# Four graph layers on one core: the scaled table rows of layers 1 and 2 made by ACT, tile by tile, in place of Pool's products

## What is computed

```python
edge_index = jnp.stack([src, dst])
x = _layernorm(x + _L0_gnn_ref(x, src, dst, edge_weight), axis=-1)
x = _layernorm(x + _L1_gnn_ref(x, src, dst, ...), axis=-1)
x = _layernorm(x + _L2_gnn_ref(x, src, dst), axis=-1)
x = _layernorm(x + _L3_gnn_ref(x, edge_index, ...), axis=-1)
```

```python
# layer 1: _gcn_conv, then a mixture of experts and a batch norm
norm = inv_sqrt[edge_src] * inv_sqrt[edge_dst]
agg = segment_sum(feats[edge_src] * norm[:, None], edge_dst)
# layer 2
xs = x * norm_in[:, None]
h = segment_sum(xs[s], d) * norm_out[:, None]
```

## Time and profile before

| | |
|---|---|
| median of 3 runs | 7959.14 us (7951.74 to 7964.05) |
| the profiled execution | 7969.68 us, span in the profile 7968.1 us |
| TensorE clock granted, mean | 0.811 |
| PE busy / POOL busy | 5263.4 us (66%) / 5261.4 us (66%) |
| DVE busy / ACT busy | 3827.5 us (48%) / 1977.2 us (25%) |
| boundary 1 | from about 3270 to 3349 us |
| boundary 2 | from about 5446 to 5549 us |

### The profile page before, as it was taken

How to read it: one execution, slowest core, us unless ns; L and a number is a source line. 1 busy time by engine, 2 the same in 40 slices (tenths; PEclk the granted TensorE clock), 3 DMA queues, 4 the chain that set the end, 5 groups by cost and what they waited for, 6 DMA issues and landing times. The chain is left out here.

```text
span 7968.1 us, 132980 instructions
## 1 busy us (share of the span) xinstructions
PE 5263.4 (66%) x33652; PEld 3720.9 (47%) x33653; DVE 3827.5 (48%) x17654; ACT 1977.2 (25%) x5480; POOL 5261.4 (66%) x4303
## 2 busy tenths in 40 slices
PE   0666666666666675088888447801888884888885
PEld 0555555555555454055444446600554443554444
DVE  4876667776777674622322553325223225223225
ACT  1333334444444442411110002302111002110003
POOL 0788888888888887266666552275666664666663
PEclk5898888898888886598899558955889985889987
DMA  9677777777667775666654105613455543455542
GB/s 213 59 74 69 72 74 82 83 89 92 95 98 101 101 105 66 227 199 210 190 168 148 34 31 155 173 45 102 150 154 168 165 156 106 151 159 164 168 153 81
DMA packets 942951, 982.36 MB, mean 123 GB/s; under 512 B 203852, under 2 KB 825779, under 8 KB 942538
## 3 DMA queue, kind: packets, MB, share of 16 engines
q0 software_dynamic: 309984, 274.81, 27.1%
q1 hardware_dynamic: 286252, 521.11, 20.6%
q10 hardware_dynamic: 346302, 181.56, 8.2%
HBM read 622.06 MB, written 337.58 MB: 120 GB/s over the span
## 5 line engine op out<-in xcount | busy, mean ns | idle before, releaser
L756 POOL DMA_INDIRECT work<-table,src_t x2169 | 2203.5, 1016 | 1127.7 <-issue 631.8
L789 POOL DMA_INDIRECT sums<-work,idx x1564 | 2478.5, 1585 | 690.8 <-issue 289.8
L1296 PE MATMUL pp<-shared 128*128 128x408 bf16 (+7 forms) x10584 | 2191.3, 357 | 703.2 <-issue 354.9
L1296 PEld LDWEIGHTS pp<-shared 128*128 128x128 bf16 x10584 | 1053.9, 105 | 1678.0 <-issue 854.0
L1727 DVE TENSOR_TENSOR acc<-acc,pp 128x80 f32 x543 | 128.4, 237 | 1921.3 <-remote 1283.0
L1278 PE MATMUL pp<-work 128*128 128x80 f32 x4338 | 659.6, 297 | 245.9 <-issue 134.3
L1278 PEld LDWEIGHTS pp<-work 128*128 128x128 f32 x4338 | 649.5, 216 | 326.1 <-issue 282.1
L1193 PE MATMUL pp<-acc 128*128 128x130 f32 x3128 | 536.8, 324 | 326.8 <-ACT work L944 269.4
L1193 PEld LDWEIGHTS pp<-acc 128*128 128x128 f32 x3128 | 469.8, 229 | 344.9 <-issue 344.9
L1015 ACT ACTIVATE shared<-shared 128x128 bf16<-128x128 f32 x588 | 179.2, 305 | 1693.3 <-DVE shared L1734 723.2
L961 ACT ACTIVATE shared<-pp 128x441 bf16<-128x441 f32 (+18 forms) x1086 | 547.4, 550 | 111.5 <-PE pp L1232 77.3
(11 more groups left out here) (316 smaller groups left out, 7105.8 us busy)
## 6 DMA issues: line engine op xcount, KB each, us to landing
shared<-counts SPq DMA_DIRECT2D x84, 840.0 KB
shared<-counts SPq DMA_DIRECT2D x42, 882.0 KB
work<-table,src_t POOLq DMA_INDIRECT x2169
shared<-counts SPq DMA_DIRECT2D x42, 819.0 KB
shared<-counts SPq DMA_DIRECT2D x42, 808.5 KB
shared<-counts SPq DMA_DIRECT2D x42, 798.0 KB
shared<-counts SPq DMA_DIRECT2D x42, 756.0 KB
shared<-counts SPq DMA_DIRECT2D x42, 714.0 KB
```

The lines of the kernel that those rows point to most:

```text
L756: pool.indirect_dma_start(out=msg[:, i % SLOTS, k, :], out_offset=None, in_=table, in_offset=bass.IndirectOffsetOnAxis(ap=src_t[:, at:at + ...
L789: pool.indirect_dma_start(out=sums0[k], out_offset=bass.IndirectOffsetOnAxis(ap=picked, axis=0), in_=rows, in_offset=None, bounds_check=NP ...
L1296: i = pe.matmul(bank[c][:, 0:COLS[n]].rearrange("p (k w) -> p k w", w=PACK * w), x3[:, b % 2, h, part3, :], ring[:, q % RING, 0:TB * COLS[ ...
```

## The change

Pool's `scale_rows` is taken out. ACT gets a new stage `scaled_rows`, which makes the same rows with seven activations of 128x128 (a Copy with a scale per partition) in place of the one product of 128x896. In ACT's order it stands one batch late, behind `deviation`: a step of ACT is now `normal_rows(b-1)`, `deviation(b)`, `scaled_rows(b-1)`. It waits for the same two signals as before, X of its batch (now ACT's own work) and the store that used the slot last. Pool has nothing left to do at boundary 1. At boundary 2 it has `shift` alone, and only two of its steps are written out ahead of its loop.

```diff
@@ Pool
-            def scale_rows(layer, scale):
-
-                def body(b, s, turn):
-                    pool.wait_ge(x_ready, layer * NB + b + 1)
-                    pool.wait_ge(tab_stored[s], 16 * ((layer + 1) * STORES + turn))
-                    pool.tensor_tensor(slot[:, 2 + s, :, :], X[:, tiles(b), :],
-                                       in_scale[:, scale, tiles(b)].unsqueeze(2).to_broadcast([P, TB, D]), ALU.mult).then_inc(tab_ready, 1)
-                return body
...
             extra_windows(pool, scatter_extra)
-            batches(pool, scale_rows(0, 0))
             gather(1)
...
-            batches(pool, shift, scale_rows(1, 1), lags=(0, 1))
+            batches(pool, shift)
@@ ACT
+            def scaled_rows(layer):
+
+                def body(b, s, turn):
+                    apart(act, x_ready, layer * NB + b + 1)
+                    act.wait_ge(tab_stored[s], 16 * ((layer + 1) * STORES + turn))
+                    for j in range(TB):
+                        i = act.activation(slot[:, 2 + s, j, :], X[:, b * TB + j, :], ACT.Copy,
+                                           scale=in_scale[:, layer, ds(b * TB + j, 1)])
+                    i.then_inc(tab_ready, 1)
+                return body
...
-            batches(act, normal_rows(0, 0), deviation(0), lags=(1, 0))
+            batches(act, normal_rows(0, 0), deviation(0), scaled_rows(0), lags=(1, 0, 1))
             gather(1)
...
-            batches(act, normal_rows(1, 0), deviation(1), lags=(1, 0))
+            batches(act, normal_rows(1, 0), deviation(1), scaled_rows(1), lags=(1, 0, 1))
             gather(2)
```

## The result

The change measured 7945.08 us (median of 9 runs, 7932.5 to 7951.1) against 7962.90 us for nine runs of the kernel before (7951.74 to 7968.72). The ratio is 0.9977, with a 95% interval of 0.9968 to 0.9985. The forecast was 7944.6 us and 0.9982: the forecast ratio lies in the interval, and so does the line of 0.2%, so these runs alone do not say on which side of it the change is.

The account below looks back on a forecast made before the run. Each boundary was taken as a chain between engines, with DVE waiting 18.6 us for Pool at boundary 2. Boundary 1 +2.2 and boundary 2 -16.7 make -14.5 us, from 7959.1 to 7944.6 us; range 7936 to 7955.

Parts of the forecast that it names:

- Boundary 2 holds 18.6 us of DVE waiting for Pool: Boundary 2: 13 steps each lose 1.43 us to Pool; steps fall from 6.53 to 5.10 us, -18.6 us.
- my 5.10: Boundary 2: DVE's step where Pool leaves it alone, in us; expected to set the step after the change.
- The shift fits over bn_stats with 0.5 us to spare: Boundary 2: shift ends over 2.3 us after y, before DVE's next two-input instruction at 2.8 us.
- A product at 0.29 us: Both boundaries: ACT's successive 128x128 products begin 0.29 us apart, within bounds of 0.26 and 0.44.
- The rivals at 0.26 and 0.44: Both boundaries, product spacing in us: 0.26 gives -18.2 us in all, chance 0.25; 0.44 gives +16 us, chance 0.06.
- ACT's step of 5.04 us at boundary 1: Boundary 1: ACT's 5.04 us exceeds DVE's 4.82 and replaces 4.98 over 13 steps, +0.8 us.
- two more waits, taken as 0.1: ACT's step: two added waits for signals already there, 0 to 0.2 us, counted as 0.1.
- 208 p: Both boundaries, ACT setting both steps: total change 208 p - 75.6 us, p being product spacing; -15.3 at 0.29.
- The ends: After the last deviation: later normalisation and last store add 1.1 and 0.3 us at boundary 1, 1.4 and 0.5 at boundary 2.
- The sum: Whole kernel: +2.2 us at boundary 1 and -16.7 at boundary 2, together -14.5 us.
- the rival that lets ACT become the bound: Both boundaries: products do not overlap, spacing 0.44 us, +16 us, 7975 us in all; loss from 0.363; chance 0.06.
- The rival with a shift that keeps blocking DVE: Boundary 2: shift starts late or Pool drifts, steps stay 6.53 us, +4 us, 7963 us in all; chance 0.10.

Follow-up runs that it names:

- doubling: The change with ACT's seven products at boundary 1 made twice, against the kernel before: 7941.82 us, ratio 1.0029.
- The first comparison: The whole change against the kernel before, nine runs each: 7945.08 against 7962.90 us, ratio 0.9977.
- the second: The whole change run again on another chip, against the kernel before at 7918.51 us there: 7905.62 us, ratio 0.9984.
- the last timeline above: The change at boundary 2 alone, with Pool's second shift held until the first y, against the kernel before: 7949.88 us, ratio 0.9983.

## Why the prediction was right

- **Boundary 2 holds 18.6 us of DVE waiting for Pool.** Right, and shown from both sides: the shift moved back brings 17.6 us of it back, and the shift left out takes 16.6 us away. The change recovered 13 x (6.53 - 5.16) = 17.8. The 0.8 missing are DVE's own loop, 5.16 for 5.10 us: my 5.10 was read from a step written out ahead of the loop, where addresses are constants, and one step of 5.42 at the entry of the loop.
- **The shift fits over bn_stats with 0.5 us to spare.** Right: it ended 0.56 us before L1854, taken from 5493.06 and 5493.62. At the two boundaries of all twelve traces, DVE's two-input instructions that began beside a wide instruction of Pool stood still for the rest of it, down to one of seven values (1.69 us for 0.17), and one-input instructions (bn_stats, the reciprocal of 0.20 us) did not. This agrees with the rule of the Trainium skill, page "SBUF — State Buffer", section "Who interferes with whom", that a DVE instruction with two SBUF inputs and a GpSimd instruction that reads SBUF contend.
- **A product at 0.29 us.** Right, 0.294 by doubling. The rivals at 0.26 and 0.44 fell. (In the first of them ACT's 4.83 us would have set the step, not DVE's 4.82, so that its -2.9 us should read -2.7.)
- **ACT's step of 5.04 us at boundary 1.** The mechanism was right, two sizes were a little off, in opposite directions. Steps with products took 4.94 to 5.02 us written out and 5.15 in the loop: the deviation and the term "two more waits, taken as 0.1" were to be 0.30 together and measured 0.21 written out and 0.40 in the loop. And the sum took 13 steps of this kind where twelve carry products; the first took 4.82 us, as before. With twelve, the prediction's own terms give +0.5 us in place of +0.8, and its formula 194 p in place of 208 p. In part the two cancel: the 13 steps average 5.08 us.
- **The ends.** Normalisation after the deviation: 2.46 us at boundary 1 and 2.38 at boundary 2, forecast 2.23, from the same 0.2 of the loop. From its end to the store: 2.46 us, as forecast, with 0.13 for the handoff to itself. Together boundary 1 cost 2.9 us (forecast 2.2), boundary 2 gave 15.8 (16.7).
- **The sum**, -14.5, against -12.8 in the traces. The first comparison gave -17.8 us and the second 0.16%, 12.9 us. The forecast lies between them. What the first gave beyond the 12.8 us lies outside the boundaries, in stretches that the change does not touch.

Of the rival that lets ACT become the bound, half came true: ACT did set the step at boundary 1, but with products at 0.294 us, far from the 0.363 at which the whole would lose. The rival with a shift that keeps blocking DVE fell: the shift did not drift, and L2121 took at most 1.093 us in the change.

## What to carry to other kernels

When two engines exclude each other, look for the place where the short work of one lies over work of the other that is not affected, and for what pushes it out of there: here a product that waited for something late, in the same queue. Moving work to a third engine pays where it empties that queue (16 us here in the traces) and costs where the receiving engine becomes the bound (3 us), so move it boundary by boundary. Read the floor of a step from inside the loop, and count the register instructions of the engine that will have no gaps left.

## What the runs showed of the hardware that was not expected

- An ACT that waits for a signal it gives itself begins 0.12 to 0.13 us after the instruction that gives it has ended (5526.36 + 2.78 = 5529.14, the next at 5529.26 in the trace, and at boundary 1 3341.16 to 3341.29). Where a deviation stands between the two, this can't be read off: in the loop the products began 0.31 us after the normalisation's end (3294.83 to 3295.14), but the deviation ran until 3295.02, and written out they began after 0.16 us.
- A DVE instruction of 0.17 us can be held for 1.69 us by one Pool instruction. In the list of costliest groups L1854 does not appear; there it shows as 41.4 us in which ACT's normalisation waited for it. Its own line's longest duration, 2.07 us against a median of 0.17, gives it away.
- The exclusion works in both directions. Before, where Pool's product began while DVE's sum was running, it was Pool that stood still, 2.32 us for 1.68:

```profile
5498.46 1.09 DVE L2125 TENSOR_TENSOR work<-work 128x896 f32<-128x896 f32 x1
5498.77 2.32 POOL L783 TENSOR_TENSOR work<-X,w_t 128x896 f32 x1 [1.29 <-ACT X L1042]
```

  At the start of boundary 2 in the last timeline above, the first shift took 2.97 us in place of 2.07, having begun 0.05 us after DVE's product.
- The gather stage of layer 1, untouched by any of these kernels, took 1096 to 1117 us in twelve profiles at mean granted clocks of 0.811 to 0.814: 1096 to 1102 in the eight on the two chips where the kernel before takes some 7919 us, 1107 and 1109 in the two on the third, and 1110 and 1117 in the first two of all. This is more than most of the effects studied here, which is why each of them was read from its own stretch.
